# LN1 from a turned copy of x, with row statistics spread through DRAM, and a third X slot

## The reference

```python
x = x + xattn(layernorm(x), ctx_1024, w_sim, b_sim, W_qv, b_qv)
x = x + ffn(layernorm(x), W1, b1, phases, w_real, w_imag, W2, b2)

# xattn (e = layernorm(x) of a batch, q = its 77 context rows)
Sim = (e @ w1)[:, :, None] + (q @ w2)[:, None, :] + einsum('bid,bjd->bij', e * w3, q) + b_sim
hq_hat = softmax(Sim, axis=2) @ q
hc_bar = softmax(max(Sim, axis=2), axis=1) weighted mean of the rows of e
out = concat([e, hq_hat, e * hq_hat, e * hc_bar]) @ W_qv + b_qv

# ffn, 512 -> 2048 -> 512
h = x @ W1 + b1
q = h + (cos(theta) * w_real + sin(theta) * w_imag) * w_imag * sin(theta + 0.1 * h) * 0.1
out = relu(q) @ W2 + b2
```

## Time and profile before

| | us |
|---|---|
| median of 3 runs | 2023.63 (2021.65 to 2024.2) |
| profiled execution, its own time | 2022.12 |
| its span, first to last instruction | 2020.3 |
| mean granted TensorE clock, as a share of full | 0.996 |

### The profile page before, as it was taken

One profiled execution on the slowest core, in us unless ns is written; L12 is line 12 of the kernel. 1 busy time (PEld: TensorE's weight loads), 2 busy tenths in 40 slices (PEclk: granted clock), 3 DMA queues, 4 the chain that ended last, 5 costly groups with the idle time before them and its releaser, 6 DMA issues.

```text
span 2020.3 us, 25250 instructions
## 1 busy us (share of the span) xinstructions
PE 1980.5 (98%) x9057; PEld 1626.0 (80%) x9057; DVE 1356.7 (67%) x2406; ACT 965.3 (48%) x1669; POOL 401.1 (20%) x834
## 2 busy tenths in 40 slices
PE   6989999999999999999999999999999999999999
PEld 5767788888888888888888888888888888888887
DVE  6777675767767577675767767567675767767554
ACT  7464543635445363543636445363543636445343
POOL 0122222212122121122212122121122212121110
PEclk9999999999999999999999999999999999999999
DMA  7375856757477574766757476574766756467473
GB/s 261 121 263 188 288 178 175 238 150 223 136 214 218 152 231 127 229 180 173 238 148 224 138 217 216 151 230 128 227 182 174 235 148 222 142 196 217 136 209 124
DMA packets 143679, 386.22 MB, mean 191 GB/s; under 512 B 24995, under 2 KB 34539, under 8 KB 143556
## 3 DMA queue, kind: packets, MB, share of 16 engines
q0 software_dynamic: 83584, 304.31, 49.9%
q1 hardware_dynamic: 59828, 80.27, 12.6%
q10 hardware_dynamic: 144, 0.04, 0.0%
HBM read 343.81 MB, written 40.76 MB: 190 GB/s over the span
## 4 chain that ended last, share of the span: by engine, by line
PE 71%; DVE 15%; ACT 7%; issue 5%; DMA 1%; SPq 0%; DVEq 0%; POOL 0%; ACTq 0%
PE acc L513 13%; PE acc L514 13%; PE acc L515 13%; PE hid L513 8%; PE hid L515 8%; PE hid L514 8%; DVE ph L1169 3%; DVE h L1159 3%; PE mis L615 3%; ACT act L877 2%; DVE kk L1167 2%; DVE st_x L1058 2%; DVE tmp_w L1221 1%; ACT L881 1%; PE mis L521 1%
## 5 line engine op out<-in xcount | busy, mean ns | idle before, releaser
L513 PE MATMUL hid<-T,w1s 128*128 128x512 f32 x1024 | 403.8, 394 | 4.9 <-DVE ws L1045 4.3
L513 PE MATMUL acc<-ws,act 128*128 128x512 f32 x1024 | 404.1, 395 | 0.0
L515 PE MATMUL hid<-T,w1s 128*128 128x512 f32 x1024 | 399.8, 390 | 0.0
L514 PE MATMUL acc<-ws,act 128*128 128x512 f32 x1024 | 399.4, 390 | 0.0
L515 PE MATMUL acc<-ws,act 128*128 128x512 f32 x1024 | 399.4, 390 | 0.0
L514 PE MATMUL hid<-T,w1s 128*128 128x512 f32 x1024 | 399.3, 390 | 0.0
L868 ACT ACTIVATE ph<-hid,hbias 128x512 f32<-128x512 f32 x256 | 176.0, 688 | 407.2 <-PE hid L515 407.2
L877 ACT ACTIVATE act<-h 128x512 fp32r<-128x512 f32 x256 | 161.9, 632 | 390.6 <-DVE h L1159 369.4
L1173 DVE SCALAR_TENSOR_TENSOR act<-h,act 128x512 fp32r<-128x512 f32 x256 | 177.3, 693 | 185.7 <-ACT act L877 185.7
L1167 DVE TENSOR_SCALAR kk<-ph 128x512 f32<-128x512 f32 x256 | 108.8, 425 | 284.0 <-ACT ph L868 284.0
L1498 POOL DMA_DIRECT2D ws<-w2x_dram x240 | 127.6, 532 | 750.1 <-PE acc L515 739.8
(11 more groups left out here) (172 smaller groups left out, 2760.2 us busy)
## 6 DMA issues: line engine op xcount, KB each, us to landing
w1s<-w1x_dram POOLq DMA_DIRECT2D x240, 512.0 KB, 4.5
ws<-w2x_dram POOLq DMA_DIRECT2D x240, 512.0 KB, 4.0
ws<-wqx_dram POOLq DMA_DIRECT2D x56, 512.0 KB, 4.5
X<-in_x SPq DMA_DIRECT2D x15, 1024.0 KB, 8.7
out_x<-X SPq DMA_DIRECT2D x15, 1024.0 KB, 4.6
xin<-in_x SPq DMA_DIRECT2D x14, 1024.0 KB, 6.8
w_raw<-in_L_ffn_W SPq DMA_DIRECT2D x32, 256.0 KB, 4.6
w1x_dram<-w1s POOLq DMA_DIRECT2D x16, 512.0 KB, 3.6
```

What stands on the lines that cost most here:

```text
L513: pe.matmul(dst, w_hi, m_hi, start=start, stop=False)
L514: pe.matmul(dst, w_hi, m_lo, start=False, stop=False)
L515: mm = pe.matmul(dst, w_lo, m_hi, start=False, stop=stop)
```

## The change

The host passes x a second time, turned: for each batch the 512 columns lie on 4 x 128 partitions and the rows along the free axis. For batches 1 to 15 this copy is loaded into `full` at f = 11. The statistics still come from the untouched X (four bn_stats per batch, now at f = 10 between the product chunks), and POOL's `deviation_first` now stands at f = 11, ahead of `deviation_second`. As mean and rstd lie one row to a partition, SP stores both in DRAM and loads them back repeated to all 128 partitions, into `mean_bc` and `e_bc` (f = 12). DVE subtracts the mean at f = 15 (`center`, two of 128x1024) and multiplies by rstd at f = 0 of the next batch (`scale`, two of 128x1024). ACT casts the four chunks to the high half of T at the top of f = 1 and 2 (`spread_high`), DVE writes the low half (`spread_low`). `tr_first`, `turned_high`, `full_copy` and `norm_first` remain for batch 0 only.

X has three slots in place of two, and `xin1` is gone: SP loads x of batch n + 1 at f = 6 of body n - 1, and that one load serves statistics and residual. `add_b2` moves to f = 4 (tiles 0, 1) and f = 8 (tiles 2, 3) of its own batch. In the opening `multiply(0)` comes ahead of `turn(1)` on PE, the load of w0 waits until the transposes of batch 0 are done (its tile holds the normalised x of batch 0 before), and in the body of batch 0 the four late `product_add` move from f = 0 and 1 to f = 3.

```diff
+    stat_dram = nc.dram_tensor("stat_dram", [2, 2, R], F32).ap()
-        X = sb("X", [P, 2, RT, D])
-        xin1 = sb("xin1", [P, RT, D])
+        X = sb("X", [P, 3, RT, D])
+        mean_bc = sb("mean_bc", [P, R])
 # SP
+            def x_load(n):
+                need(sp, out_stored, 16 * (n - 2))
+                sp.dma_start(X[:, n % 3], x_rows[n]).then_inc(x_in, 16)
+            def turned_load(n):
+                sp.wait_ge(pr_lo, C * n)
+                sp.dma_start(full[:], x_turned[n]).then_inc(xt_in, 16)
+            def spread_stats(n):
+                sp.wait_ge(rs1, n + 1)
+                sp.wait_ge(hbr_done, C * n)
+                    for k, src in ((0, mv_x[:, :, 1]), (1, rstd_x[:])):
+                        sp.dma_start(stat_dram[n % 2, k].rearrange("(t p) -> p t", p=P), src).then_inc(stat_st, 16)
+                sp.wait_ge(stat_st, 32 * n)
+                for k, dst in ((0, mean_bc[:]), (1, e_bc[:])):
+                    sp.dma_start(dst, stat_dram[n % 2, k:k + 1].to_broadcast([P, R])).then_inc(bc_in, 16)
-                    if f == 1 and n + 1 < B:
-                        xin_load(n + 1)
-                        x_load(n, pn)
+                        x_load(n + 1)
+                    if f == NA + 1:
+                        turned_load(n + 1)
+                    if f == NA + 2:
+                        spread_stats(n + 1)
 # PE
+                multiply(0)
                 turn(1)
-                multiply(0)
-                    if f == 0 and not last:
-                        tr_first(n, 0)
-                        tr_first(n, 1)
-                    if f == 1 and not last:
-                        tr_first(n, 2)
-                        tr_first(n, 3)
 # ACT
+            def spread_high(n, c, par):
+                sc.wait_ge(xs_done, 4 * n)
+                nc.scalar.copy(T[:, par, 0, c], full[:, c]).then_inc(t1_hi, 1)
                     if f in (1, 2) and not last:
-                        for t in (2 * f - 2, 2 * f - 1):
-                            turned_high(n, t, pn, tr1, t1_hi)
-                            full_copy(n, t)
+                        for c in (2 * f - 2, 2 * f - 1):
+                            spread_high(n, c, pn)
 # DVE
+            def center(n, half):
+                if half == 0:
+                    ve.wait_ge(xt_in, 16 * n)
+                    ve.wait_ge(bc_in, 32 * n)
+                cs = slice(2 * half, 2 * half + 2)
+                ve.tensor_tensor(full[:, cs], full[:, cs], mean_bc[:].unsqueeze(1).to_broadcast([P, 2, R]), ALU.subtract
+                                 ).then_inc(xs_done, 1)
+            def scale(n, half):
+                ve.wait_ge(xs_done, 4 * n - 1 if half else 4 * n - 2)
+                cs = slice(2 * half, 2 * half + 2)
+                ve.tensor_tensor(full[:, cs], full[:, cs], e_bc[:].unsqueeze(1).to_broadcast([P, 2, R]), ALU.mult
+                                 ).then_inc(xs_done, 1)
+            def spread_low(n, c, par):
+                ve.wait_ge(t1_hi, C * n + c + 1)
+                low(T[:, par, 1, c], full[:, c], T[:, par, 0, c]).then_inc(t1_lo, 1)
-                add_b2(0, 0, 0)
-                add_b2(0, 0, 1)
+                for half in range(2):
+                    center(1, half)
-                    if first and f < 2:
-                        product_add(GAP + 2 * f)
-                        product_add(GAP + 2 * f + 1)
+                    if first and f == 3:
+                        for k in range(GAP, CN):
+                            product_add(k)
-                    if f == 0:
-                        add_b2(b, par, 2)
-                        add_b2(b, par, 3)
+                    if f == 4:
+                        add_b2(b, 0)
+                        add_b2(b, 1)
+                    if f == 8:
+                        add_b2(b, 2)
+                        add_b2(b, 3)
-                    if f == FT - 1:
-                        add_b2(n, pn, 0)
-                        add_b2(n, pn, 1)
+                    if f == 0:
+                        scale(n, 0)
+                        scale(n, 1)
+                    if f == FT - 1 and n + 1 < B:
+                        center(n + 1, 0)
+                        center(n + 1, 1)
-                    if f == 3 and n + 1 < B:
-                        for t in range(RT):
-                            stats_first(n + 1, t)
-                                norm_first(n + 1, 2 * c - 4)
-                                norm_first(n + 1, 2 * c - 3)
+                                stats_first(n + 1, 2 * c - 4)
+                                stats_first(n + 1, 2 * c - 3)
 # POOL
-                    if f == 4 and n + 1 < B:
-                        deviation_first(n + 1)
                     if f == NA + 1:
+                        if n + 1 < B:
+                            deviation_first(n + 1)
                         deviation_second(n)
 # host
+    a = _np.ascontiguousarray(a.reshape(a.shape[0], a.shape[1], -1, P).transpose(0, 3, 2, 1))
+    arrays["in_x_turned"] = a
```

More of the change, by code:

```diff
@@ L341, in xattn_ffn @@
             w1_raw[:, q].rearrange("p c k -> p (c k)")[:, 0:C * CR] for q in range(2)]
-        c_product = [X[:, 1, q] for q in range(4)]
+        c_product = [X[:, 2, q] for q in range(4)]
         w1q_raw, w1q = w3_sb, T[:, 1]
+        x0n = w0_sb
         def g_source(n):
@@ L357, in _ @@
             row = lambda v, n: v.rearrange("(a d) -> a d", a=1).to_broadcast([n, D])
-            def xin_load(n):
-                sp.wait_ge(tr1, RT * n)
-                sp.dma_start(xin1[:], x_rows[n]).then_inc(xin_in, 16)
-            def x_load(n, par):
-                need(sp, out_stored, 16 * (n - 1))
-                sp.dma_start(X[:, par], x_rows[bass.ds(n, 1)].rearrange("b p t d -> (b p) t d")
-                             ).then_inc(x_in, 16)
+            def x_load(n):
[7 more added lines that the diff above has]
+                sp.wait_ge(hbr_done, C * n)
+                with nc.allow_non_contiguous_dma(reason="row statistics"):
+                    for k, src in ((0, mv_x[:, :, 1]), (1, rstd_x[:])):
[3 more added lines that the diff above has]
+                    sp.dma_start(dst, stat_dram[n % 2, k:k + 1].to_broadcast([P, R])).then_inc(bc_in, 16)
             def rows_in(k):
@@ L618, in tr_first @@
             def tr_first(n, t):
-                transpose_rows(n, t, xin1[:, t], xn1, tr1, (t2_lo, RT * n - 2 + t + 1) if t < 2 else (t1_lo, RT * n + t - 1))
+                transpose_rows(n, t, x0n[:, t], xn1, tr1, (t2_lo, RT * n - 2 + t + 1) if t < 2 else (t1_lo, RT * n + t - 1))
             def tr_second(n, t):
@@ L1218, in row_mean @@
                 for c in chunks:
-                    ve.wait_ge(full_done, RT * (n + 1))
+                    if n == 0:
+                        ve.wait_ge(full_done, RT)
+                    else:
+                        ve.wait_ge(xs_done, 4 * n)
                     need(ve, w0_lo if c == 0 else hbr_done, C * n + c)
@@ L1255, in chunk, with evacuate, attention_and_stats, norm_second @@
                 chunk_low(n, c)
-            def evacuate(par, t, done):
-                ve.tensor_tensor(X[:, par, t], X[:, par, t], acc[:, t], ALU.add).then_inc(done, 1)
-            def attention_and_stats(n, par, tiles=range(RT)):
-                if n > 0:
-                    ve.wait_ge(x_in, 16 * n)
+            def evacuate(n, t, done):
+                ve.tensor_tensor(X[:, n % 3, t], X[:, n % 3, t], acc[:, t], ALU.add).then_inc(done, 1)
+            def attention_and_stats(n, tiles=range(RT)):
                 for t in tiles:
                     ve.wait_ge(att_done, RT * n + t + 1)
-                    evacuate(par, t, x2_done)
+                    evacuate(n, t, x2_done)
                     ve.wait_ge(x2_done, RT * n + t + 1)
-                    ve.bn_stats(st[:, t], X[:, par, t]).then_inc(st2, 1)
-            def norm_second(n, par, t):
+                    ve.bn_stats(st[:, t], X[:, n % 3, t]).then_inc(st2, 1)
+            def norm_second(n, t):
                 ve.wait_ge(rs2, t // 2 + 1 if isinstance(n, int) and n == 0 else n + 2)
@@ L1314, in attention_first @@
                 for t in range(RT):
-                    norm_first(0, t)
+                    norm_first(t)
                 low_part(1)
@@ L1358, in attention_first @@
                 first_tile_low(3)
-                for t in range(RT):
-                    norm_first(1, t)
                 w1_low(0)
@@ L1387, in body @@
                     if f == 1 and not last:
-                        turned_low(n, 0, pn, full_done, t1_lo)
-                        turned_low(n, 1, pn, full_done, t1_lo)
+                        spread_low(n, 0, pn)
+                        spread_low(n, 1, pn)
                     if f == 2 and not last:
-                        turned_low(n, 2, pn, full_done, t1_lo)
-                        turned_low(n, 3, pn, full_done, t1_lo)
+                        spread_low(n, 2, pn)
+                        spread_low(n, 3, pn)
```

(8 more changed lines are left out.)

65 lines of the change are left out of this document (33 added, 32 removed).

## The result

The kernel after took 2076.23 us (median of 4 runs, 2074.75 to 2077.49), the kernel before on the same chip 2023.47: ratio 1.0261, 95% interval 1.0248 to 1.0274. It is slower, as forecast, but by 52.8 us where 18.3 were forecast, and outside the range. The profiled execution took 2074.75 us, with a granted clock of 0.988 (0.996 before).

A forecast was written before the change was run, and what follows sets the result against it. It took PE's stream and a DVE/ACT chain ending together at f = 9 as the bound: 14 steady batches x 1.13 = 15.8, batch 0 3.0, opening -0.5, so 2023.6 + 18.3 = 2042 us; range 2012 to 2056.

The forecast's parts named there:

- The steady batch: Batches after batch 0: PE's 1.74 us saving given back, at_s later on DVE, net +1.13 us a batch, 15.8 for 14.
- Both causes: Scale at f = 0 delays sim_rows, giving back 1.74 us; add_b2 at f = 8 delays at_s by 1.29 us.
- the forecast's signs: Signs of being right: batch about 122.4 us, PE waits of 1.3 or more at sim_rows, 1.5 for at_s.
- Its first rival: Whole kernel: PE bounds and the DVE/ACT chain has room, so 26.1 us are gained, 1997.5 us; chance 0.12.
- Rival 2: Steady batch: scale cheap enough for sim_rows, only f = 8 bites; net -0.6 us a batch, 2018 us; chance 0.14.
- Rival 3: Statistics too late for center once both DMA legs exceed 26.5 us; at 30 us, 2095 us; chance 0.06.
- batch 0 and the opening: Batch 0, set by DVE: +3 us, between -2 and 6; opening: 0, at most 1 us gained, counted as -0.5.
- Sum 3.7: DVE's surplus in batch 0: add_b2 at f = 4 and 8, 1.29 us each, center at f = 15 about 1.1.
- 26.5 us of room: Statistics' DRAM round trip, from about 320 us to center at 346.5: hidden; two loads of 12.7 us would still fit.
- Rival 4: New PE waits also lower the granted clock: 1.7 us a batch, 24 us more, 2066 us; chance 0.05.

The follow-up runs named there:

- e5_store16: Kernel after, statistics stores meant to write 16-byte pieces (done for one of each pair); rows return in another order, so time alone counts: 2063.02 us, ratio 1.0196.
- e12_flat: Kernel after, add_b2 at f = 13 and 14, scale at f = 15, SP's wait and loads behind raw weights, turn(1) first, 4-byte stores from GpSimd: 2028.60 us.
- e1b_split: Kernel after, SP's wait for the statistics stores and the broadcast loads moved behind the raw weight loads; repeated for its trace: 2067.77 us.
- e9_poolq: Kernel after, statistics stores issued by GpSimd behind deviation_first, SP's wait and broadcast loads behind the raw weight loads: 2057.82 us, ratio 1.0167.
- e13_flat0: As e12_flat, but with scale at f = 0, where the change puts it: 2030.93 us, ratio 1.0036.
- e15_pcenter: As e12_flat, but GpSimd does center for batches 3 to 15, VectorE only scale: 2033.29 us, ratio 1.0051.
- e7_early: Kernel after, statistics' round trip earlier, center and scale at f = 13, add_b2 at f = 15 and 14, SP's wait behind raw weights, opening order restored: 2097.66 us.

## Why the prediction was wrong where it was

**The steady batch was right.** With the shift of 34.94 us the forecast's times can be laid on the trace: ph(1) 390.54, measured 390.47; kk(2) 397.58, measured 397.57; the bias 403.05, measured 403.05; sim_rows 403.79, measured 403.78; kk(4) 410.49, measured 410.54; e_bc 415.61, measured 415.58; at_s 438.98, measured 438.87; PE's matmul 439.72, measured 439.61. Center and scale cost 1.22 us each, as taken. Both causes were then removed one by one. PE's waits were shorter than the forecast's signs: 1.16 us at sim_rows, and 0.29 at the matmul that reads gs, where it had named 1.3 or more, and 1.26 for at_s where it had named 1.5 (its 0.45 for that wait before the change stands in no row; the earlier trace rows has 0.28). The sum was 15.8 us for 14 batches (14.7 for 13); 17.7 came over 13: 1.10 a batch in the undisturbed ones, and the rest in single batches of 122.9 to 123.5 whose cause I did not follow.

**Its first rival** (PE bounds, 1997.5 us) fell: 13 us less of busy PE came with 52.6 us more of span. The Trainium skill, "Perfetto Trace Analysis", section "Identifying the Most-Contended Engine", advises to optimise the most-contended engine first, and judges TensorE by its weight loads, not by its busy matmuls. Here both point to PE (80% and 98%, DVE 67%), and work taken off it did not pay. Even in the best variant, with add_b2 and the stores out of the way, only 0.62 of the 1.74 us a batch are left as gain (121.27 against 120.65). Rival 2 fell too: sim_rows waited in every batch. Rival 3 did not come: the round trip took 20.1 to 22.7 us in the steady batches, not over 26.5.

**The step that failed is batch 0 and the opening**: "Sum 3.7; part may vanish behind a load, so I take 3, between -2 and 6", and "0, at most 1 us gained". They measured 32.7 up to the start of batch 1, and 34.9 with most of that batch. Behind it stands the sentence on the cover of the round trip: "26.5 us of room", with only ctx_load looked for behind it on SP. The room for center itself was there. But the wait was weighed only for what needs the statistics, not for what stands behind the waiting instruction in the queue, and in batch 0 these are the raw weight tiles, on which all engines live at that point. The forecast asked that question in the steady batch, where the answer is harmless, and did not ask it again for batch 0, whose queue is another one. Nor did it see that a DMA of 2 KB in 4-byte pieces slows the transfers beside it, in both queues: 16.6 of the 21.5 us remained when SP's own wait was out of the way. The price of a store, taken as at most 12.7 us from the earlier trace rows, was 10.1 in the median and 19.1 in just that place.

**The smaller parts.** Of the other 13 us of start, the opening lost 2.1 us where a gain was forecast (hidden(0) of batch 0 starts at 90.15 in place of 88.06), PE's waits in the attention of batch 0 grew (7.24 us for at_s, against 6.08 in the earlier trace rows; 4.99 for the first w1s at 100.78, where there was none, and 5.81 for gs at 111.16, against 3.63), and the clock fell with the stall: 0.73 granted over the 15 us behind it, and 0.86 from 93 to 263 us, against 0.95 from 93 to 230 us before. Part of the first 8.0 us is the opening's own round trip, which has the same raw loads behind it: SP stores there at 72.07 and 72.48 and waits until 83.18. With fewer pieces (e5_store16) the first pair of batch 0 stands at 210.65, 2.7 us earlier. How the rest divides between the opening's load order and add_b2 in batch 0 no run told apart. The best variant still reaches f = 13 of batch 1 14.5 us late; its trace shows 7.26 us for at_s in batch 0, 3.44 for a weight tile at 210.71, whose raw load took 14.9 us, and 8.68 at the start of batch 1, where before had 4.28. Rival 4 (clock lost by the new waits) did not come in the steady part: 1.00 granted from 263 us on, and 0.50 us for the matmul at 439.61, as before. deviation_second ended 3.4 us later and made norm_second wait 0.9 us a batch, which cost nothing, as forecast.

**No version beat the kernel before.** The best, e12_flat, is 0.25% slower: 8 us gained over 13 batches against 14.5 lost at the start. The change trades 1.74 us of PE for 2.9 us more of DVE ((1400.3 - 1356.7) / 15) in the very steps in which DVE feeds PE, and each way tried to move that work (later, earlier, onto GpSimd) met another limit.

## What to carry to other kernels

When work moves off the busiest engine onto another, lay the new work on the timeline of the receiving engine between two points that PE fixes: that gave the steady price here to a tenth of a microsecond. A wait put into an in-order queue is to be priced by what stands behind it, in each phase of the kernel that has its own order, the first pass above all. And a tiny DMA is not a cheap one: look at every transfer that is under way beside it, in other queues too, and see that none of them is urgent.

## What the runs showed of the hardware

- A store of 2 KB in 512 pieces of 4 bytes, issued by SP, landed after 8.9 to 19.1 us in after (median 10.1); a 256 KB load right behind it took 18.8 us in e1b_split, where the median is 4.9. Two stores that GpSimd issued in its own queue beside it took 17.2 and 19.1 us, against 4.4 and 6.8 in before.
- Such a store counted 528 packets when SP issued it and 32 when GpSimd did, and none of the latter took over 11.5 us (e9_poolq, e12_flat, e13_flat0, e15_pcenter).
- The whole way of a row statistic, from the store's issue to the end of the repeated load, took 28.5 us in e7_early (459.35 to 487.83). In the same batch of e12_flat it was 19.5: the stores issued at 455.57, the last load at 466.32 and landed at 475.07.
- A tensor_tensor of 128x1024 with one operand at a stride of 16 bytes, all in runs of 128, took 1.98 us on DVE in place of 1.22. With an operand repeated over two chunks it took 1.22, where two of 128x512 without repetition took 1.28.
- The same operation took 2.69 us on GpSimd, and two DVE operations beside it took 4.12 in place of 1.29 us (1.31 for the first, 2.89 for the second).
